# Biases added by accumulating DMAs, and the context's sum gathered by DMAs in a one-core sequence-mixer layer

## What is computed

```python
def mixer(x, W_omega, b_omega, log_scale, ln_gamma, ln_beta, W1, b1, W2, b2):
    omega = einsum('bsd,ed->bse', x, W_omega) + b_omega
    position = arange(1, S + 1)
    phi = cumsum(omega * exp(log_scale) / sqrt(position), axis=1)
    cm_real, cm_imag = x * cos(phi), x * sin(phi)
    mem_real = cumsum(cm_real, axis=1) / position
    mem_imag = cumsum(cm_imag, axis=1) / position
    ret_real = mem_real * cos(phi) + mem_imag * sin(phi)
    ret_imag = mem_imag * cos(phi) - mem_real * sin(phi)
    context = concatenate([cm_real, cm_imag, ret_real, ret_imag], axis=-1)   # 1024 values a row
    h = layernorm(context) * ln_gamma + ln_beta
    h = gelu(einsum('bsd,ed->bse', h, W1) + b1)
    return x + einsum('bsd,ed->bse', h, W2) + b2

x = x + mixer(layernorm(x), ...)
h = relu(einsum('bsd,fd->bsf', layernorm(x), sign_weights(ffn_W1)) + ffn_b1)
out = x + einsum('bsf,df->bsd', h, sign_weights(ffn_W2)) + ffn_b2
```

## Time and profile before

| | before |
|---|---|
| median of 3 runs | 1588.15 us (1587.58 to 1589.06) |
| the profiled execution | 1588.53 us, span 1586.7 us |
| PE busy | 1500.4 us, 95% of the span |
| DVE busy | 1396.1 us, 88% |
| ACT busy | 1251.9 us, 79% |
| POOL busy | 499.5 us, 31% |
| queue of POOL's accumulating DMAs | 50.34 MB, 19.1% of 16 engines' span |
| queue of SP's and ACT's DMAs | 69.51 MB, 17.2% |

### The profile page before, as it was taken

How to read it: one execution, slowest core, us unless ns; L and a number is a source line. 1 busy time by engine, 2 the same in 40 slices (tenths; PEclk the granted TensorE clock), 3 DMA queues, 4 the chain that set the end, 5 groups by cost and what they waited for, 6 DMA issues and landing times.

```text
span 1586.7 us, 30356 instructions
## 1 busy us (share of the span) xinstructions
PE 1500.4 (95%) x10937; PEld 905.7 (57%) x10937; DVE 1396.1 (88%) x2334; ACT 1251.9 (79%) x1775; POOL 499.5 (31%) x331
## 2 busy tenths in 40 slices
PE   3789999999999999999999999999999999999994
PEld 2455556656555665655566565556656555665662
DVE  6989999999998999999999999999989999998831
ACT  6768887887887878898887889788778887877743
POOL 1222333333233333223333322333332233333210
PEclk9789999999999999999999999999999999999997
DMA  5223433343444334344333434433343442333212
GB/s 205 54 54 71 90 80 70 79 94 67 81 94 75 72 81 88 73 81 94 72 76 81 85 76 80 94 71 77 81 79 83 81 94 64 77 74 72 62 28 53
DMA packets 200579, 125.45 MB, mean 79 GB/s; under 512 B 140272, under 2 KB 190704, under 8 KB 200432
## 3 DMA queue, kind: packets, MB, share of 16 engines
q0 software_dynamic: 26112, 50.34, 19.1%
q1 hardware_dynamic: 172688, 69.51, 17.2%
q10 hardware_dynamic: 1632, 3.67, 0.6%
HBM read 23.87 MB, written 33.55 MB: 36 GB/s over the span
## 4 chain that ended last, share of the span: by engine, by line
PE 56%; DVE 30%; issue 9%; ACT 2%; DMA 1%; SPq 1%; DVEq 0%; POOL 0%; POOLq 0%; ACTq 0%
PE ps L903 16%; PE ps L934 11%; PE ps L953 10%; PE ps L918 9%; PE ps L863 5%; DVE arena L1258 3%; DVE mr L1193 3%; DVE xs L1126 3%; DVE mi L1181 2%; DVE ph L1149 2%; DVE rr L1224 2%; DVE mr L1205 2%; DVE bn L1082 2%; PE ps L876 2%; DVE bn L1277 1%
## 5 line engine op out<-in xcount | busy, mean ns | idle before, releaser
L903 PE MATMUL ps<-arena,w_hi 128*128 128x512 f16 x2048 | 610.3, 380 | 1.5 <-DVE arena L1234 1.2
L903 PE MATMUL ps<-arena,w_lo 128*128 128x512 f16 x1024 | 388.7, 380 | 0.0
L903 PEld LDWEIGHTS ps<-arena,w_hi 128*128 128x128 f16 x2048 | 198.1, 98 | 223.6 <-issue 3.6
L918 PE MATMUL ps<-turned,fw_t 128*128 128x512 f16 x1024 | 253.7, 382 | 33.3 <-DMA turned<-rows 17.0
L934 PE MATMUL ps<-fw_t,arena 128*128 128x256 f16 x2048 | 254.9, 273 | 0.5 <-DVE arena L1302 0.4
L682 ACT ACTIVATE arena<-ps,relu_bias,relu_scale 128x512 f32<-128x512 f32 x256 | 191.5, 772 | 60.1 <-PE ps L918 60.1
L934 PEld LDWEIGHTS ps<-fw_t,arena 128*128 128x128 f16 x2048 | 199.8, 98 | 58.7 <-ACT arena L691 2.1
L519 POOL TENSOR_TENSOR sqr<-sqr,turn 128x1024 f32<-128x1024 f32 x32 | 88.1, 2755 | 344.4 <-ACT sqr L630 329.5
L1302 DVE TENSOR_TENSOR arena<-arena 128x512 f16<-128x512 f32 x256 | 169.4, 682 | 25.4 <-ACT arena L691 25.0
L953 PE MATMUL ps<-w_hi,arena 128*128 128x256 f16 x1024 | 183.4, 273 | 0.0
L918 PEld LDWEIGHTS ps<-turned,fw_t 128*128 128x128 f16 x1024 | 97.4, 98 | 137.3 <-DVE arena L1258 29.6
(11 more groups left out here) (193 smaller groups left out, 2703.2 us busy)
## 6 DMA issues: line engine op xcount, KB each, us to landing
x_rows<-in_L_attn_x SPq DMA_DIRECT2D x32, 512.0 KB, 4.1
rr<-qa POOLq DMA_DIRECT2D x32, 512.0 KB, 5.1
ri<-qb POOLq DMA_DIRECT2D x32, 512.0 KB, 5.4
out<-x SPq DMA_DIRECT2D x32, 512.0 KB, 2.9
out<-x POOLq DMA_DIRECT2D x32, 512.0 KB, 5.9
arena<-in_L_attn_W ACTq DMA_DIRECT2D x1, 2048.0 KB, 11.4
arena<-in_L_ffn_W SPq DMA_DIRECT2D x2, 1024.0 KB, 11.1
turned<-rows SPq DMA_TRANSPOSE x128, 2.4
```

Source lines behind the costliest of these rows:

```text
L903: last = pe.matmul(ps[:, 4 + m], w[:, k, m * P:(m + 1) * P], a[:, c.b, k], start=(i == 0), stop=(i == len(passes) - 1))
L918: last = pe.matmul(ps[:, 4 + m % KE], fw1_t[:, k, m * P:(m + 1) * P], a[:, k], start=(i == 0), stop=(i == len(passes) - 1))
```

## The change

Four things change.

1. **Biases.** `bias_pieces`, `BIAS_GROUP` and the eight bias matmuls a chunk go. SP loads the two biases, repeated on all partitions, into `bias_rows`. POOL adds `b2` to `base` (`base_bias`, behind ACT's `base_scaled`) and `f_b2` to `x1` (`x1_bias`, behind ACT's `normalise_2`) by accumulating DMAs from SBUF to SBUF, one each a chunk. `mixer_residual` waits for the first, SP's store of `x1` for the second; that store moves from the front of SP's step to behind the first transposes.
2. **The context's sum.** SP copies `cmr` into `cs` (`gather`, at the end of its step), POOL adds `cmi`, `rr` and `ri` to it by three accumulating DMAs (`gather_rest`), each waiting for the one before, ahead of `square_sums`. DVE adds the two halves of `cs` into `sqr[:, 1]` (`context_sum`, ahead of `phase_sums`), so that `sqr` holds the squares and the sum. ACT rounds both at once into `cs` (`sums_hi`, now behind `output`), DVE subtracts (`sums_lo`, behind `phase_sums`), and `context_stats` has 16 one-column matmuls. `square_lo` on POOL goes. `cosine` waits for the statistics of the chunk before, since it writes `cs`.
3. **Order.** DVE's fourth `scale_hidden` stands ahead of the two retrieval products.
4. **Memory.** `xs` shares its bytes with `qb`, with waits for that in `normalise_1` and `product_real_sin`.

```diff
+        xs = qb[:, :, :].rearrange("p k n -> p (k n)").rearrange("p (t d) -> p t d", d=D)
...
-        q_hi = sqr[:, 1, 0:CH // 2].bitcast(F16)
-        q_lo = sqr[:, 1, CH // 2:CH].bitcast(F16)
+        sum_halves = cs[:, :, :].bitcast(F16).rearrange("p h (k n) -> p h k n", k=2)
+        sums_h, sums_l = sum_halves[:, 0], sum_halves[:, 1]
...
+            def gather(c):
+                need(sp, cmr_done, c)
+                need(sp, ra_done, c)
+                need(sp, rb_done, c)
+                sp.dma_start(cs[:, :, :], cmr[:, :, :]).then_inc(copied, 16)
+
             def step(s):
-                if c := s.chunk(0):
-                    need(sp, x1_done, c)
-                    sp.dma_start(out_v[c.index], x1[:, c.b]).then_inc(stored[c.b], 16)
...
+                if c := s.chunk(0):
+                    need_dma(sp, x1_biased, c)
+                    sp.dma_start(out_v[c.index], x1[:, c.b]).then_inc(stored[c.b], 16)
+                if (c := s.chunk(2)) and c.index:
+                    gather(c)
+
...
+            def base_bias(c):
+                need(pool, scaled_done, c)
+                pool.dma_start(base[:, c.b], b2_rows, accum_op=ALU.add).then_inc(base_biased[c.b], 16)
+
+            def x1_bias(c):
+                need(pool, xs2_done, c)
+                pool.dma_start(x1[:, c.b], f_b2_rows, accum_op=ALU.add).then_inc(x1_biased[c.b], 16)
...
                     output_sum(before)
-                if nxt:
-                    square_lo(nxt, ahead)
                 if far:
                     inverse_std_1(far)
+                if ahead:
+                    base_bias(ahead)
+                if now:
+                    x1_bias(now)
                 if nxt:
                     inverse_std_context(nxt)
                 if ahead:
                     product_imag_sin(ahead)
                     retrieve(ahead)
+                    gather_rest(ahead)
                     square_sums(ahead)
...
-            def square_lo(c, after):
-                if after:
-                    need(pool, frac_done, after)
-                need(pool, q_done, c)
-                need(pool, qh_done, c)
-                pool.tensor_tensor(q_lo, sqr[:, 0], q_hi, ALU.subtract).then_inc(ql_done, 1)
+            def gather_rest(c):
+                need(pool, cmi_done, c)
+                need_sum(pool, copied, c)
+                pool.dma_start(cs[:, :, :], cmi[:, :, :], accum_op=ALU.add).then_inc(gathered, 16)
+                need_sum(pool, rr_done, c)
+                need_gathered(pool, 1, c)
+                pool.dma_start(cs[:, :, :], rr[:, :, :], accum_op=ALU.add).then_inc(gathered, 16)
+                need_sum(pool, ri_done, c)
+                need_gathered(pool, 2, c)
+                pool.dma_start(cs[:, :, :], ri[:, :, :], accum_op=ALU.add).then_inc(gathered, 16)
...
             def normalise_1(c):
                 need(act, t1_done, c, 1) if c.index < 3 else need(act, l1_done, c, 3)
                 need(act, lean1_done, c)
+                if c.index > 1:
+                    need_sum(act, ri_done, c, 2)
...
                 need(act, abs_done, c)
+                need(act, stats_done, c, 1)
                 act.activation(cs[:, :, :], turn[:, :, :], ACT.Sin, scale=-TWO_PI,
                                bias=half_pi[:, 0:1]).then_inc(cos_done, 1)
...
             def sums_hi(c):
                 need(act, q_done, c)
-                act.copy(q_hi, sqr[:, 0]).then_inc(qh_done, 1)
+                need(act, sum_done, c)
+                act.copy(sums_h, sqr[:, :, :]).then_inc(sums_h_done, 1)
...
+                if before:
+                    output(before)
                 if nxt:
                     sums_hi(nxt)
-                if before:
-                    output(before)
...
             def context_stats(c, after):
-                for part in range(4):
-                    need(pe, ch_done[part], c)
-                    need(pe, cl_done[part], c)
                 if after:
                     need(pe, u_done, after)
-                for j in range(NT):
-                    halves = [(a, k) for k in range(KC) for a in (ch, cl)]
-                    for i, (a, k) in enumerate(halves):
-                        pe.matmul(ps[:, 3, j:j + 1], a[:, c.b, k, j * P:(j + 1) * P], ones_h[:, 0:1],
-                                  start=(i == 0), stop=(i == len(halves) - 1))
-                need(pe, qh_done, c)
-                need(pe, ql_done, c)
-                for j in range(NT):
-                    for src in (q_hi, q_lo):
-                        last = pe.matmul(ps[:, 3, NT + j:NT + j + 1], src[:, j * P:(j + 1) * P], ones_h[:, 0:1],
-                                         start=(src is q_hi), stop=(src is q_lo))
+                need(pe, sums_h_done, c)
+                need(pe, sums_l_done, c)
+                for i in range(2):
+                    for j in range(NT):
+                        for src in (sums_h, sums_l):
+                            last = pe.matmul(ps[:, 3, (1 - i) * NT + j:(1 - i) * NT + j + 1], src[:, i, j * P:(j + 1) * P],
+                                             ones_h[:, 0:1], start=(src is sums_h), stop=(src is sums_l))
                 last.then_inc(stats_done, 1)
...
                 if m == 0:
                     need(pe, out_done, c, 1)
-                    for j in range(NT):
-                        pe.matmul(ps_rows_a[:, j], ones_h[:, :], bias_row[:, 1], start=(j % 2 == 0), stop=False,
-                                  skip_group_check=True)
                 need_block(pe, rh_done, m, c)
                 need_block(pe, rl_done, m, c)
                 for j in range(NT):
                     for a in (rh, rl):
                         last = pe.matmul(ps_rows_a[:, j], a[:, m % SLOTS, j * P:(j + 1) * P], fw2_t[:, m],
-                                         start=False, stop=(m == KF - 1 and a is rl),
+                                         start=(m == 0 and j % 2 == 0 and a is rh), stop=(m == KF - 1 and a is rl),
...
                 for j in range(NT):
-                    pe.matmul(ps_rows_b[:, j], ones_h[:, :], bias_row[:, 0], start=True, stop=False)
                     passes = [(a, w, m) for m in range(KE) for a, w in ((gh, w2_hi), (gh, w2_lo), (gl, w2_hi))]
                     for i, (a, w, m) in enumerate(passes):
                         last = pe.matmul(ps_rows_b[:, j], a[:, m, j * P:(j + 1) * P], w[:, m],
-                                         start=False, stop=(i == len(passes) - 1))
+                                         start=(i == 0), stop=(i == len(passes) - 1))
...
+                if c.index:
+                    dve.wait_ge(l1_done, min(c.index, CHUNKS - 2))
+                else:
+                    dve.wait_ge(t1_done, 2)
                 dve.scalar_tensor_tensor(out=qb[:, :, :], in0=mr[:, :, :], scalar=-1.0, in1=sn[:, :, :],
                                          op0=ALU.mult, op1=ALU.mult).then_inc(qb_done, 1)
...
+            def context_sum(c):
+                need_gathered(dve, 3, c)
+                need(dve, q_done, c)
+                dve.tensor_tensor(sqr[:, 1], cs[:, 0], cs[:, 1], ALU.add).then_inc(sum_done, 1)
+
+            def sums_lo(c):
+                need(dve, sums_h_done, c)
+                dve.tensor_tensor(sums_l, sqr[:, :, :], sums_h, ALU.subtract).then_inc(sums_l_done, 1)
...
             def mixer_residual(c):
                 need(dve, w2_done, c)
-                need(dve, scaled_done, c)
+                need_dma(dve, base_biased, c)
...
                     first_rows_lo(far)
                 if ahead:
                     memory_real(ahead)
+                if nxt:
+                    scale_hidden(nxt, 3)
+                if ahead:
                     retrieve_imag_cos(ahead)
                     retrieve_real_cos(ahead)
-                if nxt:
-                    scale_hidden(nxt, 3)
...
+                if ahead:
+                    context_sum(ahead)
                 if far:
                     phase_sums(far)
+                if ahead:
+                    sums_lo(ahead)
```

More of the change, by code:

```diff
@@ L198, in phase_mixer_layer @@
         wo_in = h2.rearrange("p k n -> p (k n)").bitcast(F32).rearrange("p (m d) -> p m d", m=KD)
-        bias_cols = l2.rearrange("p k n -> p (k n)").bitcast(F32).rearrange("p (i q) -> p i q", q=P)
+        b2_rows, f_b2_rows = (bias_rows[:, i].unsqueeze(1).to_broadcast([P, NT, D]) for i in range(2))
         ps = ctx.enter_context(nc.psum_tensor("ps", [P, 8, CH], F32))
@@ L250, in phase_mixer_layer @@
         added = [sem(f"added{i}") for i in range(2)]
+        base_biased = [sem(f"base_biased{i}") for i in range(2)]
+        x1_biased = [sem(f"x1_biased{i}") for i in range(2)]
         bn1_done, mv1_done, ve1_done = sem("bn1_done"), sem("mv1_done"), sem("ve1_done")
@@ L344, in need_sum, with need_gathered @@
             wait(eng, s, c.counts.value(16, 16 * (c.more + 1 - back)))
+        def need_gathered(eng, parts, c):
+            wait(eng, gathered, 48 * c.index + 16 * parts)
```

(33 more changed lines are left out.)

36 lines of the change are left out of this document (13 added, 23 removed).

## The result

The changed kernel takes 1741.79 us (1737.95 to 1743.9) against 1587.91 before: a ratio of 1.0965, 95% interval 1.0945 to 1.0985. The forecast was 1637 us with a range up to 1690: the sign was right, but the time lies above the range, and the growth, 154 us, was three times the 49 that the sum gave. The profiled execution has a span of 1740.2 us, 153.5 more than before.

The account below looks back on a forecast made before the run. The prediction took the gather's DMA chain, closed over the step, as the bound: 1588.5 us, plus 7 for start and end, plus 30 chunks x (47.8 - 46.4) = 42, giving 1637 us, range 1582 to 1690.

Parts of the forecast that it names:

- The gather's chain: Copy, three accumulating DMAs and POOL's squares ahead of context_sum set the period: 47.8 us a chunk, chance 0.62.
- the marks named for this case: DVE waiting about 2 us before context_sum, accumulations in sequence on POOL, PE waiting for turned rows, omega and z-block waits gone.
- the copy's landing: SP's copy of cmr into cs, issued 27.2 us after the phase sums start, lands 4.1 us later, at 31.3.
- far end: Slow case for the copy of cmr, landed at 33.5 instead of 31.3; with links of 5.4 to 5.7, 50.6 us a chunk.
- the fourth transpose: Last of SP's first transposes, beside the rr accumulation: lands after 5.2 us, its neighbour 2.5; used to stretch the copy's time.
- The first link: POOL's accumulation of cmi into cs, overlapping ri's: 5.4 us to landing plus 0.3 for POOL's answer.
- the floor: DVE alone allows 45.7 us a chunk, with 1.3 us of waiting for omega gone because PE gets ahead.
- the first rival: The gather hides, with copy and accumulations at their cheapest: 45.7 to 45.8 us a chunk, 1576 us, chance 0.13.
- the start: First chunk: DVE waits 8 us at context_sum, removed bias_pieces return 2.5; second chunk adds 4 us.
- The bias accumulations: Rival: base_bias and x1_bias DMAs delay SP's second transposes by 2.7 us: 48.3 us a chunk, 1652 us, chance 0.15.
- The clock: Rival: PE idles about 4 us a chunk and its granted clock stays low longer: about 1700 us, chance 0.05.
- the edits that were priced at nothing: cosine's new wait, xs in qb's place, output ahead of sums_hi, square_lo leaving POOL: no cost expected.

Follow-up runs that it names:

- rr and ri cut: Changed kernel with the accumulations into rr and ri reduced to 128 of 1024 columns, the rest left out: 1660.89 us.
- The copy placed first: Changed kernel with SP's copy of cmr issued ahead of the store of x1 instead of behind it: 1746.97 us.
- two links: Changed kernel without the third accumulating DMA, so ri is not in the context's sum: 1606.22 us.
- the biases alone: Kernel before with biases added by accumulating DMAs, the later x1 store and xs in qb's bytes; context's sum stays on PE: 1564.85 us, ratio 0.9845.
- the addition on DVE: Changed kernel with DVE adding cmr and cmi into cs behind product_real_sin, replacing SP's copy and the first accumulating DMA: 1621.13 us.
- the sums alone: Changed kernel with biases left to PE's matmuls and x1's store at the front of SP's step: 1697.55 us.

## Why the prediction was right and wrong

**Right: what binds.** The gather's chain set the period, closed over context_sum, and everything that PE got rid of (145 us of waiting stand ahead of its spread) was worth nothing. Three of the marks named for this case are in the rows: the wait ahead of the 128x512 addition, released by POOL's squares or the last part, though of 3.2 us and not 2; the links one behind the other on POOL; the wait for the z block gone. Two are not: PE has hardly a wait for the turned rows (it waits for the statistics instead), and DVE's wait for omega is still there.

**Wrong: the copy's landing, the step I had said I trust least.** I took 4.1 us from a load that runs beside one accumulation, with 33.5 - 27.2 = 6.3 as the far end. The far end is what came, 6.3 to landing, and 6.88 to POOL's answer: 2.5 of the 3.4 us that the period is over the forecast. (How the 6.3 follows from the fourth transpose is not worked out in the prediction: stretched as that one is, by 5.2 / 2.5, the store's 2.9 would become 6.0 and the load's 4.1 would become 8.5.) The first link, 5.7, was short by 0.7. Both errors are one: I priced each transfer as a latency of its own and not the set as an amount of work. A first number to do it with was in the table of before: POOL's queue had 19.1% of 1586.7 us, 303 us, for 3 x 32 accumulations, a mean of 3.16 us of all 16 engines for each. The windows of one step (us, busy us and counts of PE, PEld, DVE, ACT, POOL, granted clock, DMA share, GB/s) show it:
```profile
800.00:820.00 20.00, 14.54 (x62) 6.58 (x61) 19.42 (x34) 18.20 (x26) 7.95 (x5) 0.83 0.68 122
822.00:830.00 8.00, 7.97 (x59) 5.48 (x58) 8.00 (x12) 7.71 (x13) 0.88 (x1) 1.00 1.03 254
830.00:836.00 6.00, 6.00 (x49) 4.53 (x47) 4.85 (x6) 4.62 (x6) 0.86 (x1) 1.00 0.49 94
837.00:841.00 4.00, 4.00 (x31) 2.81 (x30) 3.05 (x11) 1.11 (x1) 0.28 (x1) 1.00 0.69 131
848.00:853.00 5.00, 4.08 (x34) 1.91 (x33) 4.90 (x9) 3.87 (x6) 0.31 (x1) 1.00 0.77 105
```
The second link runs alone between 837 and 841: 0.69 x 4 = 2.76 us of all 16 engines for 512 KB from SBUF to SBUF. The accumulation into `out` runs alone between 848 and 853: 0.77 x 5 = 3.85. The 3.16 is about the mean of two of the one kind and one of the other. While POOL waits for the copy (822 to 830), all 16 DMA engines are full: rr's and ri's additions alone are 5.5 us, and the copy, the store and the last transposes come on top. So the copy, issued at 821.71, is answered when that amount is through. Behind 830 the engines are half idle (0.49), and in this step the first link takes 5.69, as forecast; its mean of 6.39 falls to 5.61 with rr and ri cut. The copy placed first moved the time into the link, and with rr and ri cut it went: that settles it for 3.0 of the 3.2 us. The 3.2 us that the Trainium skill's fit gives for 512 KB (DMA: Bandwidth & Descriptors, section "Anatomy of one DMA — SWDGE (gpsimd) path") is short of the 4.5 of a link that runs alone; the measurement decides.

The prediction's own far end, 50.6 us a chunk, is near the 51.17 that came; by its sum it gives 1588.5 + 7 + 30 x 4.2 = 1721.5 us, and the range stopped at 1690, short of it.

**Wrong: the floor.** I let the wait for omega go "since PE gets ahead", 45.7. It is 27.9 us in 27 chunks after, 24.3 with two links and 35.5 with the biases alone. My reading, from PE's order alone: omega follows mixer_out, which needs the last part of gelu_lo from the same step, so PE cannot get ahead of DVE there; no run isolates it. The kernel with two links runs at 46.84, and the one with the addition on DVE at 47.34, which less its 1.14 would be 46.2. This did not move the forecast, but it takes the ground from the first rival: by these two runs a gather that hides would have run at 46.2 to 46.8 us, about as before or slower, and not at 45.7. No run hides the whole gather, so the floor itself stays open.

**Wrong by 3.3 us: the start.** In the first chunk the wait was to be 8 us; it was 11.34 (timelines of POOL and DVE):
```profile
65.15 0.86 POOL L551 DMA_DIRECT2D cs<-rr  x1 [4.55 <-DMA cs<-cmi]
72.15 0.86 POOL L554 DMA_DIRECT2D cs<-ri  x1 [6.14 <-DMA cs<-rr]
```
```profile
76.83 0.69 DVE L1261 TENSOR_TENSOR sqr<-cs 128x512 f32<-128x512 f32 x1 [11.34 <-POOL sqr L543]
```
The second link took 72.15 - 65.15 = 7.0 us instead of 4.8. The load of x_rows was issued just before it, at 64.92; whether that is the cause was not tried.

**The other rivals.** The bias accumulations do not hold up the transposes by an amount that counts (the biases alone); with the store's move they cost 1.6 us a chunk in the gather (the sums alone), which the prediction had at nothing. The clock: between 800 and 820 the granted clock is 0.83, part of the time at the lower of the two levels (1.2 GHz), and 1.00 in the windows behind. It was at the lower one between 807 and 812 (0.50), when PE waited for the statistics, 5.5 us up to 809.43, and in the matmuls that follow. DVE's wait for the matmuls that follow (L1288) is 12.2 us in all, 0.4 a chunk. That is the size of the 0.3 by which the copy goes out late; whether it is the clock or PE's late start is not shown.

**The rest** held: the second link, the squares, the sum and rr's product came within 0.5 us of the forecast, and at the edits that were priced at nothing, cosine, base and x1, DVE and PE have no wait that counts.

## What to carry to other kernels

Add up what a new chain's transfers and their neighbours take of all DMA engines before you price each by its latency: the queue's share of the page divided by its issues is a first number for that (a mean over kinds: 3.16 us here, for 2.76 and 3.85), and where the sum nearly fills the window, the slowest landing seen is the likely one. A chain of accumulating DMAs costs some 5 us a link here where it runs alone, and 6.4 to 8.8 where it overlaps other transfers; it must have that much room between the last producer and the first reader. Take the half of a change that only removes work (the biases), and leave the half that trades 1.4 us of work on the full engine for a chain across three others.

## What was not expected of the hardware

- An elementwise operation on POOL holds an operation of DVE, and the reverse: 0.74 us became 3.25 beside 2.68 us of POOL, two scans 2.5 became 3.9 beside the additions of the squares, POOL's 1.27 became 2.11. In the changed kernel these additions of the squares cost DVE nothing, as it stands still then.
- An accumulating DMA of 512 KB takes 2.76 us of all 16 engines from SBUF to SBUF and 3.85 into `out`, and a transfer issued from another queue beside two of them is late too: x1's store went from 2.9 to 5.5 us to landing by moving from the front of SP's step to its end, beside rr's and ri's additions, and to 5.7 with the biases alone, without a gather.
